# A fused FFN, attention, FFN block: a new order for the work of its opening

## The chip, the cores and the metric

The kernel runs on all 8 cores of one Trainium2 chip. Every core runs the same program on its own 2 of the 16 sequences, and the cores do not talk to each other. The metric is the device time in microseconds (us) of the slowest core. TensorE is called PE below, VectorE DVE, ScalarE ACT, GpSimd POOL; SP is the engine that issues most of the DMAs.

## What is computed

For x of 16 sequences of 2048 rows of 1024 (f32), with normalised rows h = layernorm(x):

```python
x = x + 0.5 * ffn(layernorm(x))      # ffn: h @ W_shared.T + w(h) * (h @ W_expert.T) + bias
x = x + attention(layernorm(x))      # 16 heads of 64, causal, softmax, output product Wp
x = x + 0.5 * ffn(layernorm(x))
```

In the FFN every row goes to two experts that share one matrix, so that the expert part is a scale per row (from a gate of 7 columns, softmax, top 2) times the same product. The scales of the two experts add up to 1, and the kernel multiplies with the sum of W_shared and W_expert.

## The kernel before

**Tiles and chunks.** A core has 4096 rows: 32 tiles of 128 rows, in 8 chunks of 4 tiles. Chunks 0 to 3 are one sequence, 4 to 7 the other. A tile is loaded (`ld`, SP), its statistics taken (`st`, DVE), its reciprocal deviation computed (`rt` for a tile, `r` for a chunk, ACT), the rows normalised (`a`, DVE or ACT), the FFN bias added to x (`xf`, POOL), and the normalised tile transposed (`t`: by PE with an evacuation copy for the first chunks, else by a DMA transpose that SP issues). Then come the gate (`ga`, `gb`), the FFN products (`f`, two halves of 512 columns to a tile), statistics of the new x (`s1`), the store of it (`sx`, SP), and the second normalisation and transposes (`a`, `t` with layer 1). A chunk's attention inputs are 8 products `q`, 8 `k` and 8 `v`; each is 8 matmuls of 512 columns, a DVE evacuation, and a store to memory. `n`, `b1` and `b2` make a bound for the exponent from the squares of q and k; the first attention step of a chunk can't do without it.

**Weights.** 48 pieces of 512 KB come through staging slots by SP (`wl`). Pieces 0 to 15 are pairs of FFN weights that DVE or POOL adds into WF (`ws`, 8 of them; 4 and 5 on POOL); pieces 16 to 23 are Wq, 24 to 31 Wk, 32 to 39 Wv, cast to bf16 by ACT or, for the numbers in `ON_POOL`, by POOL (`wc`). A slot's next piece is issued only when the last user of the slot is done, and that `wl` stands right behind the `ws` or `wc` in the order.

**One order for all engines.** `a_order` and `c_order` write out by hand the order of everything but attention; `make_order` puts the attention steps (`qd`), their loads (`al`), and the pieces of products around them (`pt` computes a product up to so many of its 8 matmuls) between them, by estimated costs of its own. Each engine walks through this one list `ORDER`, does the entries that are its own, and waits in line wherever an entry isn't ready. So an entry that waits on SP or DVE holds up all that stands behind it there. In the list `aux[k]` are the entries behind product k of a chunk (0 to 7 q, 8 to 15 k, 16 to 23 v). The attention loads `al` of units 0 to 3 stand ahead of the fifth q product of chunk 1, each as three DMAs, and wait for all q, k and v stores of chunk 0.

**Buffers.** Before the first attention step the products and PE transposes share 7 PSUM banks in turn; after it banks 6 and 7. q and k results go through 4 buffers `QKS`, v through 3 `VST`; each buffer waits for its last store to land. On ACT in chunk 0, each q or k store is issued before the cast that follows it in the list.

Of the kernel before, what the change touches and what calls it, by code (L numbers as in the profile page):

```python
# [17 lines left out]
DCN = 8  # L18
# [56 lines left out]

ON_POOL = (17, 19, 21, 23)


def ffn_order(l, i):
# [16 lines left out]
def a_order():  # L98

    o = [("ld", n) for n in range(4)] + [("bl", 0)] + [("wl", j) for j in range(8)]  # L100
# [3 lines left out]
    def one_cast():  # L104
        if cast:
            j = cast.pop(0)
            o.extend([("wc", j)] + [("wl", k) for k in range(40) if WPREV[k] == j])

    def ws(j):
        o.extend([("ws", j)] + [("wl", k) for k in range(40) if WPREV[k] == 2 * j or WPREV[k] == 2 * j + 1])  # L110
# [13 lines left out]
    o += [("pt", ("f", 0, n, 0), 6) for n in range(4)]  # L124
    o.append(("gb", 0, 0))
    ws(3)
    o += [("br", 1), ("br", 2)]
    for n in range(4):
        o += [("st", n + 4), ("rt", 0, n + 4), ("a", 0, n + 4)]
        if n:  # L130
            o.append(("f", 0, n - 1, 0))
    ws(4)
    o.append(("xf", 0, 4))
    ws(5)
    o += [("xf", 0, 5), ("f", 0, 3, 0), ("t", 0, 4), ("t", 0, 5), ("xf", 0, 6), ("t", 0, 6), ("xf", 0, 7), ("t", 0, 7)]
    o += [("s1", n, 0) for n in range(4)] + [("ga", 0, 1)]
    o += [("bb", r, h) for r in (1, 2) for h in range(2)]
    o += [("gb", 0, 1)] + [("f", 0, n, 0) for n in range(4, 8)]
    o += [("pt", ("f", 0, n, 1), 4) for n in range(4)]
    ws(6)  # L140
    o += [("pt", ("f", 0, n, 1), 6) for n in range(4)]
    ws(7)
    for n in range(4):
        o += [("f", 0, n, 1), ("s1", n, 1), ("rt", 1, n)]
        one_cast()
        if n < 3:
            o.append(("a", 1, n))
            one_cast()
    o += [("f", 0, 4, 1), ("f", 0, 5, 1), ("t", 1, 0), ("t", 1, 1), ("a", 1, 3)]
    one_cast()  # L150
    o += [("f", 0, 6, 1), ("t", 1, 2), ("t", 1, 3), ("f", 0, 7, 1)]
    one_cast()
    for i in range(NCHUNK):
        aux = {k: [] for k in range(24)}
        if i == 0:
            for t in range(4):
                aux[t] += [("s1", 4 + t, 0), ("s1", 4 + t, 1)]
                aux[6 + t] += [("a", 1, 4 + t), ("t", 1, 4 + t)]
                aux[12 + t].append(("ld", 8 + t))
            aux[4].append(("r", 1, 1))  # L160
            for n in range(8):
                aux[2 + n].append(("sx", 0, n))
        elif i == 1:
            for t in range(4):
                aux[4 + t].append(("st", 8 + t))
                aux[9 + t] += [("a", 0, 8 + t), ("xf", 0, 8 + t), ("t", 0, 8 + t)]
            aux[8].append(("r", 0, 2))
            for t in range(2):
                aux[6 + t].append(("ld", 12 + t))
                aux[13 + t].append(("st", 12 + t))  # L170
            aux[14].append(("ga", 0, 2))
            aux[15].append(("gb", 0, 2))
        elif i < 7:
            aux[1].append(("r", 1, i + 1))
            for t in range(4):
                aux[2 + t] += [("a", 1, 4 * i + 4 + t), ("t", 1, 4 * i + 4 + t)]
# [29 lines left out]
        for k, e in enumerate(order if i != 1 else order[:16]):  # L206
            o.append(e)
            one_cast()
            o += aux[k]
            if k == 9:  # L210
                o.append(("n", 0, i))
            if k == 17:
                o.append(("n", 1, i))
            if k == 19:
                o.append(("b1", i))
            if k == 21:
                o.append(("b2", i))
        if i == 1:

            v = order[16:]  # L220
            for t in range(4):
                n = 8 + t
# [205 lines left out]
ORDER = make_order()  # L428
# [11 lines left out]
EARLY = [0] * 8  # L440
_uses = [0] * 8
_banks = (6, 7, 0, 1, 2, 3, 4)
_turn = 0
for _e in ORDER:
    if _e[0] == "pt":
        _e = _e[1]
    if _e == ("qd", 0):
        EARLY = list(_uses)
        _banks = (6, 7)
    elif _e == ("oe", NUNIT - 1):  # L450
        _banks = (6, 7, 0, 1, 2, 3, 4, 5)
    if _e[0] in ("bb", "t", "ga", "f", "q", "k", "v", "n", "b2", "bc", "p") and not by_dma(_e) and _e not in SHARED:
        _b = _banks[_turn % len(_banks)]
        _turn += 1
        SHARED[_e] = (_b, _uses[_b])
        _uses[_b] += 1
ATTENDED = {_e for _e in ORDER[ORDER.index(("oe", NUNIT - 1)):] if _e in SHARED}

ON_DVE = {("t", 0, 4), ("t", 0, 5)} | {("t", 1, _n) for _n in range(4)}

ON_ACT = {("a", 0, _n) for _n in range(4, 8)} | {("a", 1, _n) for _n in range(3)}


XNUSE = {}
# [14 lines left out]
_n = [0, 0, 0]  # L479
# [16 lines left out]
def build_program():  # L496
# [22 lines left out]
    with contextlib.ExitStack() as st:  # L519
# [460 lines left out]
        def tensor_program(e):  # L980
# [68 lines left out]
            def product(en, upto):  # L1049

                kind = en[0]
                begin = done.get(en, 0)
                done[en] = upto
                if not begin:
                    bank_free(en)
# [8 lines left out]
                else:  # L1064
                    n, h = en[-2], en[-1]
                    i, t = divmod(n, 4)
# [7 lines left out]
                for dc in range(begin, upto):  # L1074
                    if kind == "f":
                        if en[1] == 0 and n == 0 and dc % 2 == 0:
                            summed(e, 4 * h + dc // 2)
                        a = xt(2 * en[1], i)[:, dc, t * 128:(t + 1) * 128]
                        b = WF[:, dc, h * 512:(h + 1) * 512]
# [367 lines left out]
```

How the kernel before makes its waits and increments, by code:

```python
        def filled(e, entry):  # L692
            b, m = SHARED[entry]
            e.wait_ge(p_sh[b], m + 1)
# [1 line left out]
        def read_out(e, entry):  # L696
            b, m = SHARED[entry]
            e.wait_ge(r_sh[b], m + 1)
# [1 line left out]
        def transposed(e, entry):  # L700
            if entry in TDMA:
                b, m = TDMA[entry]
                e.wait_ge(d_t[b], 16 * m)
            else:
                read_out(e, entry)
# [21 lines left out]
        def summed(e, j):  # L728
            e.wait_ge(v_ws, j + 1 - 2 * (j > 5) - (j - 3) * (3 < j < 6))
            if j > 3:
                e.wait_ge(g_ws, min(2, j - 3))
# [1 line left out]
        def sum_pieces(e, j):  # L734
            h, m = divmod(j, 4)
            a, b = 2 * j, 2 * j + 1
            for p in (a, b):
                e.wait_ge(d_wl[WSLOT[p]], 16 * (WUSE[p] + 1))
            return e.tensor_tensor(WF[:, 2 * m:2 * m + 2, h * 512:(h + 1) * 512],
                                   piece(a).rearrange("p (c f) -> p c f", c=2),
                                   piece(b).rearrange("p (c f) -> p c f", c=2), ALU.add)
# [1 line left out]
        def cast(e, j):  # L744
            m = sum(p <= j for p in ON_POOL)
            if j - 15 - m:
                e.wait_ge(a_wc, j - 15 - m)
            if m:
                e.wait_ge(g_wc, m)
# [1 line left out]
        def cast_piece(e, j, copy):  # L752
# [4 lines left out]
                cast(e, j - 1)
            e.wait_ge(d_wl[WSLOT[j]], 16 * (WUSE[j] + 1))
            return copy(dst, piece(j))
# [36 lines left out]
            def const(instr):  # L797
# [1 line left out]
                instr.then_inc(g_c, 1)  # L799
                n += 1
                e.wait_ge(g_c, n)
```

## Time and profile before

| | |
|---|---|
| time, median of 3 runs | 1239.21 us (1237.67 to 1243.95) |
| the profiled execution | time 1238.26 us, span of its slowest core 1236.7 us |
| spans of the 8 cores | 1225.8 to 1236.7 us; core 5 is the slowest, core 1 has 1232.7 |
| busy on that core | PE 93%, ACT 60%, DVE 56%, POOL 43% |

The span runs from a core's first to its last instruction; the time is 1.6 us above it. Products are matmuls at line 1091 of the kernel: `WF,XT` for the FFN, `XT,WQKV` for q and k (the moving operand is the transposed x), `WQKV,XT` for v. Line 1114 is a PE transpose, 1133 the gate, 1143 the sum of squares `n`, 1150 the matmul of `b2`, 1010, 1033 and 1041 are attention, 1171 are statistics, 1200 and 1328 the normalisation on DVE and ACT, 942 a DMA transpose, 904 the load of x, 897 the load of a weight piece, 910 the store of x.

### The profile page before, as it was taken

Reading aid. Unit: us, or ns where it says so; the run is one execution under the profiler, and the core shown is the slowest. Engines: PE = TensorE matmul, PEld = TensorE weight load, DVE = VectorE, ACT = ScalarE, POOL = GpSimd, SP = SyncE. Lnnn points to the kernel's source line nnn. Section 1 sums busy time; section 2 is a strip of 40 time slices with the busy share of each in tenths; the row PEclk is TensorE's granted clock in tenths of the full one; section 3 lists DMA queues with packets and bytes.
Section 4 is the critical chain, followed back from the end, with each engine's and each line's share of the span. In section 5 each row is a group of like instructions: output and inputs, shape, how many; then the busy total and the mean of one; then the engine's idle time right before and its main releaser. Section 6 shows DMA issues by size and latency. Waiting matters only on the chain.

```text
span 1236.7 us, 28817 instructions; the slowest of 8 cores (1225.8 to 1236.7 us)
## 1 busy us (share of the span) xinstructions
PE 1149.8 (93%) x9038; PEld 430.1 (35%) x9038; DVE 695.4 (56%) x1239; ACT 740.1 (60%) x937; POOL 531.7 (43%) x794
## 2 busy tenths in 40 slices
PE   4789887998999999999999999999989999999997
PEld 2334333332333333333333333333333333333343
DVE  6674678765555455544545545446655545455465
ACT  3362134466667676677667556667767777777711
POOL 5633554356035405603531534725536271716352
PEclk9899999998999999999999999999999999999999
DMA  8989659697357447537544646746666664847142
GB/s 278 323 268 280 158 108 190 149 238 198 90 134 217 118 127 213 122 128 157 151 128 129 148 118 173 207 115 171 133 190 165 212 175 143 215 110 240 26 162 86
DMA packets 206760, 206.93 MB, mean 167 GB/s; under 512 B 127251, under 2 KB 171795, under 8 KB 206614
## 3 DMA queue, kind: packets, MB, share of 16 engines
q1 hardware_dynamic: 198560, 200.85, 60.6%
q10 hardware_dynamic: 8054, 4.25, 1.3%
q8 instruction: 78, 1.28, 0.4%
q14 instruction: 68, 0.56, 0.2%
HBM read 117.23 MB, written 66.85 MB: 149 GB/s over the span
## 4 chain that ended last, share of the span: by engine, by line
PE 76%; DVE 9%; issue 5%; DMA 4%; SPq 2%; ACT 2%; DVEq 0%; ACTq 0%; POOL 0%; POOLq 0%
PE PS L1091 47%; PE PS L1033 11%; PE PS L1010 11%; PE PS L1041 4%; DMA XC<-x 2%; DVE BNS L1171 2%; PE PS L1155 1%; DVE VST L1253 1%; DVE ATT L1278 1%; SPq L942 1%; DMA XT<-XN 1%; DMA qd<-QKS 1%; DVE QKS L1242 1%; DVE DSB L1285 1%; DVE XC L1227 1%
## 5 line engine op out<-in xcount | busy, mean ns | idle before, releaser
L1382 ACT ACTIVATE PT<-PS,MB 128x1024 bf16<-128x1024 f32 (+3 forms) x428 | 401.2, 988 | 150.8 <-PE PS L1010 150.1
L855 POOL TENSOR_TENSOR SQ<-QKS 128x256 bf16<-128x256 bf16 x256 | 166.1, 671 | 232.4 <-DVE QKS L1242 199.1
L1091 PE MATMUL PS<-XT,WQKV 128*128 128x512 bf16 x1024 | 247.5, 387 | 9.5 <-DVE QKS L1242 7.2
L1091 PE MATMUL PS<-WF,XT 128*128 128x512 bf16 x1024 | 247.8, 387 | 2.5 <-DVE VST L1253 2.3
L1382 ACT ACTIVATE ATT<-PS,MB 128x1024 bf16<-128x1024 f32 x212 | 193.6, 964 | 70.0 <-PE PS L1010 69.9
L869 POOL TENSOR_TENSOR OTT<-OS,RR 128x256 bf16<-128x256 f32 x124 | 89.2, 739 | 326.4 <-ACT RR L1393 326.4
L1010 PE MATMUL PS<-ATT 64*128 64x512 bf16 (+3 forms) x1280 | 177.6, 350 | 1.6 <-ACT PT L1382 0.9
L825 POOL TENSOR_TENSOR XC<-XC,BF 128x256 f32<-128x256 f32 x192 | 135.5, 736 | 63.6 <-DVE XN L1200 63.6
L1091 PEld LDWEIGHTS PS<-XT,WQKV 128*128 128x128 bf16 x1024 | 92.6, 99 | 148.0 <-issue 56.3
L1091 PEld LDWEIGHTS PS<-WF,XT 128*128 128x128 bf16 x1024 | 92.8, 99 | 141.2 <-issue 49.9
L1091 PE MATMUL PS<-WQKV,XT 128*128 128x512 bf16 x512 | 122.8, 380 | 9.2 <-DVE VST L1253 8.1
L1227 DVE SCALAR_TENSOR_TENSOR XC<-PS,GG,XC 128x512 f32<-128x512 f32 x96 | 71.7, 749 | 92.7 <-PE PS L1091 92.0
L1033 PE MATMUL PS<-PT,ATT 128*32 128x512 bf16 (+3 forms) x1712 | 118.9, 354 | 0.2 <-DVE PT L1278 0.2
L1171 DVE BATCH_NORM_STATS2 BNS<-XC 128x6 f32<-128x512 f32 x156 | 104.4, 688 | 16.4 <-DMA XC<-x 7.3
L1010 PEld LDWEIGHTS PS<-ATT 64*128 64x128 bf16 x1280 | 45.9, 93 | 135.5 <-issue 133.4
L1242 DVE TENSOR_SCALAR QKS<-PS,BK 128x512 bf16<-128x512 f32 x64 | 48.0, 750 | 72.7 <-PE PS L1091 66.3
L1253 DVE TENSOR_TENSOR VST<-PS,BV 128x512 bf16<-128x512 f32 x64 | 44.0, 688 | 79.2 <-PE PS L1091 76.3
L1242 DVE TENSOR_SCALAR QKS<-PS,BQ 128x512 bf16<-128x512 f32 x64 | 47.8, 748 | 64.1 <-PE PS L1091 60.7
L1041 PE MATMUL PS<-PT,ONES 128*32 128x512 bf16 (+3 forms) x856 | 81.3, 350 | 0.0
L1391 ACT ACTIVATE RR<-PS 128x512 f32<-128x512 f32 x64 | 38.2, 597 | 70.3 <-PE PS L1155 69.6
L1091 PEld LDWEIGHTS PS<-WQKV,XT 128*128 128x128 bf16 x512 | 44.7, 97 | 76.7 <-issue 31.8
L1285 DVE CAST DSB<-PS 128x512 bf16<-128x512 f32 x64 | 44.2, 690 | 46.4 <-PE PS L1041 45.3
(107 smaller groups left out, 1080.0 us busy)
## 6 DMA issues: line engine op xcount, KB each, us to landing
XC<-x SPq DMA_DIRECT2D x30, 512.0 KB, 7.2
x1d<-XC SPq DMA_DIRECT2D x30, 512.0 KB, 5.3
XC<-x1d SPq DMA_DIRECT2D x18, 512.0 KB, 7.4
out<-XC SPq DMA_DIRECT2D x18, 512.0 KB, 3.4
ATT<-qd SPq DMA_DIRECT2D x64, 128.0 KB, 3.9
ATT<-kd SPq DMA_DIRECT2D x16, 512.0 KB, 5.5
ATT<-vd SPq DMA_DIRECT2D x16, 512.0 KB, 6.3
od<-OTT SPq DMA_DIRECT2D x62, 128.0 KB, 3.4
```

The costliest lines, as they stand in the source:

```text
L825: i = e.tensor_tensor(x[:, f:f + 256], x[:, f:f + 256], b[:, f:f + 256], ALU.add)
L855: i = e.tensor_tensor(SQ[:, m % 8, f], q[:, f], q[:, f], ALU.mult)
L869: m = e.tensor_tensor(to[:, f], OS[:, u % 2, f], RR[:, u % 2, f], ALU.mult)
L1010: i = e.matmul(PS[:, S_BANK + 2 * m + h, off:512], kk[64 * h:64 * h + 64, (j + m) * 128:(j + m + 1) * 128], q[64 * h:64 * h + 64, off:512] ...
L1033: e.matmul(PS[32 * g:32 * g + 32, O_BANK, off:512], vv[:, v + 32 * g:v + 32 * g + 32], ptile(k)[:, 2 * m + g // 2, off:512], start=(j + m ...
L1041: i = e.matmul(PS[32 * g:32 * g + 32, D_BANK, off:512], ONES[:, 0:32], ptile(k)[:, 2 * m + h, off:512], start=(j == 0 and (m == 0 or c > 0 ...
L1091: m = e.matmul(sbank(en), a, b, start=(dc == 0), stop=(dc == DCN - 1))
L1171: m = e.bn_stats(BNS[:, b, 6 * h:6 * h + 6], xtile(l, n)[:, h * 512:(h + 1) * 512])
L1227: i = e.scalar_tensor_tensor(x, sbank(en), GG[:, n // 4 % 2, n % 4:n % 4 + 1], x, ALU.mult, ALU.add)
L1242: was_read(e.tensor_scalar(QKS[:, m % NQK, :], sbank(en), bias[:, hp:hp + 1], None, ALU.add), en)
L1285: e.tensor_copy(DSB[:, u % 2, :], PS[:, D_BANK, :]).then_inc(v_ds, 1)
L1382: e.activation(ptile(k)[:, 2 * m:2 * m + 2, off:512], PS[:, S_BANK + 2 * m:S_BANK + 2 * m + 2, off:512], AF.Exp, bias=MB[:, u // HPN, hp % ...
```

## The change

The opening of `a_order` is written anew. FFN products of tiles 0 to 3 are issued whole as parts ahead of their evacuations; tiles 4 to 7 are normalised one by one between those (tiles 4 and 6 on ACT, 5 and 7 on DVE, instead of all four on ACT); the second halves of tiles 0 to 3 are begun as soon as their weights come, ahead of the gate and the first halves of tiles 4 to 7; casts 18 and 22 go to POOL. 8 casts stand ahead of the first q product instead of 9, and the first four q products have two casts behind each instead of one. The broadcasts `bb` of two bias rows move from the opening to products 10 to 13. The third chunk (tiles 8 to 11) is loaded three products sooner, its statistics move from q products 4 to 7 of chunk 1 to behind products 15, 17, 19 and 21 of chunk 0, its normalisation and DMA transposes from products 9 to 12 of chunk 1 to products 1 to 4, and its gate from product 14 to product 8. The loads of tiles 12 and 13 move from products 6 and 7 of chunk 1 to 20 and 22 of chunk 0, their statistics to products 10 and 12. Of the 7 PSUM banks the one whose last user ends first in the list is taken, not the next in turn.

```diff
--- before.py
+++ after.py
@@ -75,7 +75,7 @@
 
 
 
-ON_POOL = (17, 19, 21, 23)
+ON_POOL = (17, 18, 19, 21, 22, 23)
 
 
 def ffn_order(l, i):
@@ -124,52 +124,68 @@
     o += [("pt", ("f", 0, n, 0), 6) for n in range(4)]
     o.append(("gb", 0, 0))
     ws(3)
+
+    def parts(products, m):
+
+        o.extend(("pt", p, m) for p in products)
+
+    half = [("f", 0, n, 1) for n in range(4)]
+    parts([("f", 0, n, 0) for n in range(4)], 8)
     o += [("br", 1), ("br", 2)]
-    for n in range(4):
-        o += [("st", n + 4), ("rt", 0, n + 4), ("a", 0, n + 4)]
-        if n:
-            o.append(("f", 0, n - 1, 0))
+
+    o += [("st", 4), ("rt", 0, 4), ("a", 0, 4), ("xf", 0, 4), ("f", 0, 0, 0)]
+    o += [("st", 5), ("rt", 0, 5), ("t", 0, 4), ("f", 0, 1, 0), ("a", 0, 5), ("xf", 0, 5), ("t", 0, 5)]
+    o += [("st", 6), ("rt", 0, 6), ("a", 0, 6)]
     ws(4)
-    o.append(("xf", 0, 4))
+    o += [("f", 0, 2, 0), ("st", 7), ("rt", 0, 7), ("t", 0, 6), ("f", 0, 3, 0), ("a", 0, 7)]
     ws(5)
-    o += [("xf", 0, 5), ("f", 0, 3, 0), ("t", 0, 4), ("t", 0, 5), ("xf", 0, 6), ("t", 0, 6), ("xf", 0, 7), ("t", 0, 7)]
-    o += [("s1", n, 0) for n in range(4)] + [("ga", 0, 1)]
-    o += [("bb", r, h) for r in (1, 2) for h in range(2)]
-    o += [("gb", 0, 1)] + [("f", 0, n, 0) for n in range(4, 8)]
-    o += [("pt", ("f", 0, n, 1), 4) for n in range(4)]
     ws(6)
-    o += [("pt", ("f", 0, n, 1), 6) for n in range(4)]
+    o += [("xf", 0, 6), ("t", 0, 7), ("s1", 0, 0), ("s1", 1, 0)]
+    parts(half, 2)
+    o += [("ga", 0, 1), ("xf", 0, 7)]
     ws(7)
-    for n in range(4):
-        o += [("f", 0, n, 1), ("s1", n, 1), ("rt", 1, n)]
+    parts(half, 4)
+    parts(half, 6)
+    o += [("s1", 2, 0), ("s1", 3, 0), ("gb", 0, 1)]
+    parts(half, 8)
+    one_cast()
+    one_cast()
+    parts([("f", 0, 4, 0), ("f", 0, 5, 0)], 8)
+
+    o += [("f", 0, 0, 1), ("s1", 0, 1), ("rt", 1, 0), ("a", 1, 0)]
+    o += [("f", 0, 1, 1), ("s1", 1, 1), ("rt", 1, 1), ("t", 1, 0)]
+    one_cast()
+    parts([("f", 0, 6, 0)], 8)
+    o += [("f", 0, 2, 1), ("s1", 2, 1), ("a", 1, 1), ("rt", 1, 2), ("a", 1, 2)]
+    one_cast()
+    o += [("f", 0, 3, 1), ("s1", 3, 1), ("rt", 1, 3), ("t", 1, 1)]
+    parts([("f", 0, 7, 0)], 8)
+    o += [("t", 1, 2), ("a", 1, 3), ("t", 1, 3)]
+    for k in range(4):
         one_cast()
-        if n < 3:
-            o.append(("a", 1, n))
-            one_cast()
-    o += [("f", 0, 4, 1), ("f", 0, 5, 1), ("t", 1, 0), ("t", 1, 1), ("a", 1, 3)]
-    one_cast()
-    o += [("f", 0, 6, 1), ("t", 1, 2), ("t", 1, 3), ("f", 0, 7, 1)]
-    one_cast()
+    o += [("f", 0, n, 0) for n in range(4, 8)] + [("f", 0, n, 1) for n in range(4, 8)]
     for i in range(NCHUNK):
         aux = {k: [] for k in range(24)}
         if i == 0:
             for t in range(4):
                 aux[t] += [("s1", 4 + t, 0), ("s1", 4 + t, 1)]
+                aux[10 + t].append(("bb", 1 + t // 2, t % 2))
                 aux[6 + t] += [("a", 1, 4 + t), ("t", 1, 4 + t)]
-                aux[12 + t].append(("ld", 8 + t))
+                aux[9 + t].append(("ld", 8 + t))
+                aux[15 + 2 * t].append(("st", 8 + t))
             aux[4].append(("r", 1, 1))
             for n in range(8):
                 aux[2 + n].append(("sx", 0, n))
+            aux[20].append(("ld", 12))
+            aux[22].append(("ld", 13))
         elif i == 1:
+            aux[0].append(("r", 0, 2))
             for t in range(4):
-                aux[4 + t].append(("st", 8 + t))
-                aux[9 + t] += [("a", 0, 8 + t), ("xf", 0, 8 + t), ("t", 0, 8 + t)]
-            aux[8].append(("r", 0, 2))
+                aux[1 + t] += [("a", 0, 8 + t), ("xf", 0, 8 + t), ("t", 0, 8 + t)]
+            aux[8].append(("ga", 0, 2))
+            aux[9].append(("gb", 0, 2))
             for t in range(2):
-                aux[6 + t].append(("ld", 12 + t))
-                aux[13 + t].append(("st", 12 + t))
-            aux[14].append(("ga", 0, 2))
-            aux[15].append(("gb", 0, 2))
+                aux[10 + 2 * t].append(("st", 12 + t))
         elif i < 7:
             aux[1].append(("r", 1, i + 1))
             for t in range(4):
@@ -206,6 +222,8 @@
         for k, e in enumerate(order if i != 1 else order[:16]):
             o.append(e)
             one_cast()
+            if k < 4:
+                one_cast()
             o += aux[k]
             if k == 9:
                 o.append(("n", 0, i))
@@ -440,8 +458,9 @@
 EARLY = [0] * 8
 _uses = [0] * 8
 _banks = (6, 7, 0, 1, 2, 3, 4)
-_turn = 0
-for _e in ORDER:
+_ends = {_e: _n for _n, _e in enumerate(ORDER)}
+_until = list(range(-8, 0))
+for _n, _e in enumerate(ORDER):
     if _e[0] == "pt":
         _e = _e[1]
     if _e == ("qd", 0):
@@ -450,15 +469,16 @@
     elif _e == ("oe", NUNIT - 1):
         _banks = (6, 7, 0, 1, 2, 3, 4, 5)
     if _e[0] in ("bb", "t", "ga", "f", "q", "k", "v", "n", "b2", "bc", "p") and not by_dma(_e) and _e not in SHARED:
-        _b = _banks[_turn % len(_banks)]
-        _turn += 1
+        _b = min(_banks, key=lambda b: _until[b])
+        assert _until[_b] < _n
         SHARED[_e] = (_b, _uses[_b])
         _uses[_b] += 1
+        _until[_b] = _ends[_e]
 ATTENDED = {_e for _e in ORDER[ORDER.index(("oe", NUNIT - 1)):] if _e in SHARED}
 
-ON_DVE = {("t", 0, 4), ("t", 0, 5)} | {("t", 1, _n) for _n in range(4)}
-
-ON_ACT = {("a", 0, _n) for _n in range(4, 8)} | {("a", 1, _n) for _n in range(3)}
+ON_DVE = {("t", 0, 7), ("t", 1, 3)}
+
+ON_ACT = {("a", 0, 4), ("a", 0, 6), ("a", 1, 0), ("a", 1, 2)}
 
 
 XNUSE = {}
@@ -1050,6 +1070,8 @@
 
                 kind = en[0]
                 begin = done.get(en, 0)
+                if begin == DCN:
+                    return
                 done[en] = upto
                 if not begin:
                     bank_free(en)
```

## Rows read from the trace of the kernel before

**Rows 1.** Windows: us, busy (instructions) of PE, PEld, DVE, ACT, POOL; clock; DMA

```profile
0.00:123.00 123.00, 92.28 (x503) 43.06 (x504) 76.01 (x135) 49.67 (x85) 55.77 (x90) 0.93 0.96 289
123.00:240.00 117.00, 98.62 (x675) 40.39 (x674) 86.14 (x157) 38.76 (x70) 52.86 (x78) 0.97 0.68 148
...
400.00:600.00 200.00, 194.93 (x1624) 67.82 (x1624) 103.30 (x187) 139.37 (x160) 71.82 (x106) 1.00 0.57 152
```

**Rows 2.** PE's timeline: start, length, work [idle before and who ended it]

```profile
22.66 9.48 PE L1091 MATMUL PS<-WF,XT 128*128 128x512 bf16 x32
...
33.84 0.61 PE L1114 MATMUL PS<-IDE,XN 128*128 128x128 bf16 x8 [1.69 <-ACT XN L1328]
...
45.14 18.87 PE L1091 MATMUL PS<-WF,XT 128*128 128x512 bf16 x80
...
75.22 13.98 PE L1091 MATMUL PS<-XT,WQKV 128*128 128x512 bf16 x64
91.24 5.30 PE L1091 MATMUL PS<-XT,WQKV 128*128 128x512 bf16 x16 [2.05 <-ACT WQKV L760]
...
108.49 3.61 PE L1091 MATMUL PS<-WQKV,XT 128*128 128x512 bf16 x16 [0.93 <-ACT WQKV L760]
...
123.00 15.70 PE L1091 MATMUL PS<-XT,WQKV 128*128 128x512 bf16 x72
```

**Rows 3.** Timeline of SP's queue: start, time that the issues took

```profile
86.10 0.33 SPq L897 DMA_DIRECT2D ATT<-wtv  x1
...
107.35 2.61 SPq L904 DMA_DIRECT2D XC<-x  x4
127.56 0.33 SPq L934 DMA_DIRECT2D ATT<-qd  x1
...
134.53 0.83 SPq L904 DMA_DIRECT2D XC<-x  x2
```

**Rows 4.** DMA landing, us: 105-112 (x), 60-150 (x), 90-101 and 147-161 (transposes)

```profile
XC<-x SPq DMA_DIRECT2D x4, 512.0 KB, 11.7
...
DMA to landing us min/median/max: 6.2/9.5/12.5
...
XT<-XN SPq DMA_TRANSPOSE x3, 7.6
...
XT<-XN SPq DMA_TRANSPOSE x4, 3.1
```

**Rows 5.** PE's timeline at the start of attention and at the third chunk's gate

```profile
142.68 0.62 PE L1143 MATMUL PS<-SQ,BD 128*32 128x512 bf16 x8 [0.59 <-DVE QKS L1242]
146.37 0.81 PE L1091 MATMUL PS<-XT,WQKV 128*128 128x512 bf16 x3 [3.07 <-DVE QKS L1242]
...
166.32 0.34 PE L1133 MATMUL PS<-WGT,XT 128*128 128x7 bf16 x8 [3.58 <-DMA XT<-XN]
```

**Rows 6.** POOL's timeline in the opening

```profile
36.87 2.36 POOL L740 TENSOR_TENSOR WF<-WP 128x1024 bf16<-128x1024 f32 x1 [10.60 <-DMA WP<-wte]
39.18 2.56 POOL L825 TENSOR_TENSOR XC<-XC,BF 128x256 f32<-128x256 f32 x4
...
60.26 1.04 POOL L760 CAST WQKV<-WP 128x1024 bf16<-128x1024 f32 x1 [2.40 <-DMA WP<-wtq]
```

**Rows 7.** DVE's timeline: statistics of a tile, a v evacuation, the end of `b1`

```profile
77.89 1.28 DVE L1171 BATCH_NORM_STATS2 BNS<-XC 128x6 f32<-128x512 f32 x2
...
110.48 0.69 DVE L1253 TENSOR_TENSOR VST<-PS,BV 128x512 bf16<-128x512 f32 x1 [2.06 <-PE PS L1091]
...
117.49 0.26 DVE L1264 TENSOR_SCALAR DG<-IDE,NV 128x128 bf16<-128x128 bf16 x1
```

**Rows 8.** Window of PE alone: us, busy, granted clock, DMA share, GB/s

```profile
148.00:150.00 2.00, 2.00 (x6) 0.50 0.67 131
```

**Rows 9.** Waits of PE on core 1, 136 to 170 us: total, times, longest

```profile
PE PS L1133 <- DMA XT<-XN: 1.8, 1, 1.8
...
PE PS L1091 <- DVE QKS L1242: 0.5, 1, 0.5
```

## The prediction

> **What bounds the kernel now.** I read the table of stretches first [rows 1]. From 400 to 600 us PE is busy for 194.9 of 200 us at full clock; that is the state of nearly all of the kernel, and the change leaves it alone. Only two stretches have room: 0 to 123 us, where PE is busy for 92.3 us at a mean clock of 0.93 while the DMA engines are busy for 96%, and 123 to 240 us, where PE loses 18.4 us and DVE is busy for 74%. Because everything later is one list without slack on PE, what is won or lost on PE by 240 us should come out at the end, one for one. Next PE's own timeline [rows 2]: FFN products end their first batch at 32.1 us and go on at 45.1; between, PE does four transposes and little else. q products start at 75.2, k products wait 2.05 us for a cast, v products 0.93 us, and chunk 1 begins at 123.0 (call it S; its 72 matmuls are the 8 q products and the first k product). The third view is the queue of SP with its landings [rows 3, 4]: the loads of the third chunk's x are issued from 107.4 us only, behind the last two weight pieces (86.1), the stores of x and four DMA transposes, and they take 11.7 us to land. The fourth is PE after 138 us [rows 5].
>
> **Opening, 32 to 75 us.** Nothing of the FFN is removed; the question is how early PE gets at the second halves. They need the sum of pieces 8 and 9 on POOL, which came at 36.9 + 2.4 = 39.2 [rows 6]. In the new order two bias adds of 2.56 us stand ahead of it. Tile 4 is normalised when PE starts its transpose at 33.8 [rows 2], as now, so the sum ends at 33.7 + 2 x 2.56 + 2.36 = 41.2. From about 41.9, when the last of the four transposes is through, PE has 96 matmuls before q, 96 x 0.216 (13.98 / 64 less the pipeline's tail, [rows 2]) = 20.7 us; four transposes of 0.61, 2.4; the gate, 1.4; as much half clock as before, 1.6 (80 matmuls took 18.87 us for 80 x 0.216 = 17.3); and about 1.2 us behind the DVE copy of tile 7, which now stands behind a weight sum whose piece lands near 43.4 (landings run from 36.9 for piece 9 to 60.3 for piece 23, 1.67 us apiece [rows 6]). Sum 69.3: q starts 5.9 us sooner. The Wq pieces are in by 61.3, so they don't bind. Casts 18 and 22 on POOL cost 1.04 us each there; POOL has nothing due until the first squares, so nothing.
>
> **k and v, 75 to 109 us.** The last Wk cast is the eighth behind a q product instead of the seventh, in pairs of 2 x 1.04 us [rows 6] and 0.33 for the store's issue [rows 3]. With the first q result evacuated at 71.9, four such groups of 2.4 us end at 81.6, before k can start at 83.2 (69.3 + 13.9). That removes the 2.05 us, and what followed it: 16 matmuls took 5.30 us at low clock where 16 later took 3.61 [rows 2], 1.7 us. The v wait of 0.93 goes too. The four `bb` matmuls now cost about 1 us of dense PE time. So v can start at 108.5 - 5.9 - 3.7 - 0.9 + 1 = 99.0, up to 1.7 us later if the squares of q are late (their stores now wait behind cast pairs). Alone that would be 9.5 us. If nothing took it back, this would be the result.
>
> **What takes it back: x of the third chunk.** The statistics of tiles 8 to 11 now stand on DVE among v's evacuations, and each waits for its tile. Their loads stand in SP's queue behind two weight pieces, the stores of x and the transposes. Before, from the first weight piece (issued 86.1) to the loads (107.4) that queue took 21.2 us, since DMA was full. Now it starts near 78, when cast 28 is done, has one more 0.5 MB store (1.7 us), and so issues the first load near 97 (it has moved ahead of the last transpose) and the others at 100 to 103; with 9 to 11.7 us to land [rows 4], tile 9 is there at 110 to 113. Then DVE has, in this order: statistics of tile 9, 1.5; the `n` evacuation, 0.7; two v evacuations, 1.4; statistics of tile 10, 1.5; `b1`, 0.9 [rows 7]: 6.0 us. PE stands at `b2`, which it reaches 6 products and an `n` after v's start, at about 110, until 116 to 119. Two v products later, 3.5 us [rows 2], chunk 1 starts: tile 9 + 9.7 = 119.7 to 122.7, plus 1.8 us for the low clock after a wait of this length (as above). Middle 122.5, against 123.0. Bounds: the shortest landing of 6.2 us [rows 4] on an issue at 101.3, no clock loss: 117.2; the longest, 12.5 us on 103, with it: 127. The opening's gain is waited away for all but 0.5 us.
>
> **Start of attention.** Before, PE lost there 1.0 + 0.6 + 3.1 us waiting for k evacuations held up by q stores that landed late beside attention's loads and 1 MB of x [rows 3, 5], then 3.6 us for the last transposed tile of the third chunk at the gate, and after either a stretch at half clock [rows 8], 1.6 and 1.9 us. Together 11.8 us. The change takes the x loads away, but puts the DMA transpose of tile 11 right behind the 12 loads of `al`, which took SP from 127.56 to 134.5, 6.9 us [rows 3]. Tile 10 is normalised at S + 8.7 (four products of 1.73, the evacuation, 0.75, and the pass over the tile, 0.8), `al` is issued from S + 9.9 to S + 16.8, tile 11's transpose after it, at about S + 17. The gate now stands behind the first k product: PE is there at S + 15.7 [rows 2]. What a DMA transpose takes to land the trace shows from both sides, 3.1 us in a quiet stretch and 7.6 in a full one [rows 4]; I take 5.5, between, since `al` is still draining: S + 22.5. PE idles 6.8 us there, and at half clock loses another 1.7. In this time the stores of q land, so the old waits vanish within it: 8.5 us lost for 11.8, on this core 3.3 us better (bounds: +5.7 with 3.1 us, +1.2 with 7.6 us). On core 1 the same waits were 0.5 and 1.8 us [rows 9], some 3 us with its others: that core gets 5.7 us worse, ending at 1232.7 + 5.7. The slowest of eight is thus near 1238 from the one side and 1236.7 - 3.3 from the other; I count this part as +0.5 us (worse), with bounds of -5 and +5. The Trainium skill, DMA: Bandwidth & Descriptors, in the table of Latency and other measured facts, gives DMA transposes 261 GB/s. By it tile 11's 256 KB would be an estimated 1.0 us of transfer and the stall about 4 us shorter than mine; the 7.6 us of the trace's full stretch speak against using it while other transfers queue.
>
> **After that.** The squares of k, the gate's DVE work and two bias adds no longer meet attention's first steps; I count -1 us, out of the waits of 1 us and less there. The statistics of tiles 12 and 13 cost the same 1.5 us each wherever they stand.
>
> **Sum.** Against this execution's 1238.3 us: opening and v -0.5, attention's start +0.5, rest -1: 1237.3. The median of the three runs is 0.95 above that execution: 1238.2, which I give as 1238. What a measurement can tell from no change is about 0.5%, 6.2 us.
>
> **Rivals.**
> *The gains stay* (chance 0.30). The x tiles land with the bounds' 6 us, and tile 11's transpose in 3: 5.8 + up to 5 + 1 = some 11 us, or half of each, 7: 1228 to 1232. For it: SP's queue starts 8 us sooner. Against: four transposes and the stores still have to go through a full DMA.
> *A new wait decides, slower* (0.24). The gate's wait for tile 11: if its transpose lands more than 9 us after issue, behind `al` and q stores, PE idles over 10 us; with S no sooner than before, cores such as 1 end 9 us late: 1247. It decides from a stall of about 11 us on, 4 more than I forecast; the two waits for x add to it if tile 9 lands after 116.
> *The change of order does nothing at all for q* (inside my forecast): if PE starts q at 75 as before, v at about 104 still waits for x, and the time stays within 2 us of the forecast.
> My own case, within 0.5%, has 0.46; its own range is 1233 to 1244. For 8 in 10 both signs must be let in: 1229 to 1246.
>
> **What would show it.** Right: q at 68 to 71 us, no wait on a cast ahead of k, PE idle for over 5 us ahead of the `b2` matmul with DVE waiting for the load of x; then a gate waiting 5 to 9 us on a DMA transpose ahead of the first scores. Wrong: v evacuations that never wait for x (then S is near 113 and the time near 1228), or the gate passing without a wait.

## The result, and the profile after

The changed kernel takes 1245.58 us (median of 20 runs) where the kernel before takes 1240.01 (20 runs). The ratio is 1.0052, with a 95% interval of 1.0033 to 1.0071: slower by half a per cent. (Medians are over all runs; ratios and intervals leave out runs in which the cores of a die ran at a lower granted clock, so a ratio is not exactly the quotient of the two medians beside it.) The time is just inside the outer range of the forecast (1229 to 1246), outside the range of its own case (1233 to 1244), and the direction is not the one it gave: it had 1238 and a sum 1 us below its base.

The profiled execution took 1247.8 us, its slowest core (core 2) 1246.3. The table of stretches of that core, in the columns of [rows 1] (which show core 5 of the kernel before):

```profile
0.00:123.00 123.00, 89.43 (x500) 41.70 (x501) 83.03 (x147) 46.77 (x78) 61.93 (x92) 0.93 0.97 298
123.00:240.00 117.00, 100.74 (x674) 40.86 (x673) 78.14 (x142) 37.84 (x69) 52.07 (x78) 0.93 0.61 138
```

DVE has 7 us more to do ahead of 123 us and 8 us less behind it, as the statistics moved; PE has done no more by then. Its timeline on that core shows why; the rows answer to [rows 2] and [rows 5]:

```profile
42.40 3.62 PE L1113 MATMUL PS<-WF,XT 128*128 128x512 bf16 x8
...
69.70 17.43 PE L1113 MATMUL PS<-XT,WQKV 128*128 128x512 bf16 x80
...
99.67 3.62 PE L1113 MATMUL PS<-WQKV,XT 128*128 128x512 bf16 x16
103.22 0.62 PE L1165 MATMUL PS<-SQ,BD 128*32 128x512 bf16 x8
103.77 7.08 PE L1113 MATMUL PS<-WQKV,XT 128*128 128x512 bf16 x32
118.46 0.26 PE L1172 MATMUL PS<-DG,ONES 128*128 128x128 bf16 x1 [7.61 <-DVE DG L1286]
118.58 5.27 PE L1113 MATMUL PS<-WQKV,XT 128*128 128x512 bf16 x16
123.69 15.70 PE L1113 MATMUL PS<-XT,WQKV 128*128 128x512 bf16 x72
139.23 0.75 PE L1155 MATMUL PS<-WGT,XT 128*128 128x7 bf16 x24
146.76 0.36 PE L1155 MATMUL PS<-WGT,XT 128*128 128x7 bf16 x8 [6.78 <-DMA XT<-XN]
```

q starts at 69.7 instead of 75.2 us and v at 99.7 instead of 108.5, without a wait on a cast. Then PE stands 7.6 us ahead of the `b2` matmul, runs the next two v products at half clock (5.27 us for 16 matmuls instead of 3.62), and starts chunk 1 at 123.7, where the kernel before started it at 123.0. Behind the first k product it stands 6.8 us at the gate. What held up `b2` is on DVE's timeline:

```profile
104.10 1.29 DVE L1193 BATCH_NORM_STATS2 BNS<-XC 128x6 f32<-128x512 f32 x2 [2.76 <-DMA XC<-x]
105.49 0.21 DVE L1196 BATCH_NORM_AGGREGATE MV<-BNS 128x2 f32<-128x12 f32 x1
105.66 1.29 DVE L1275 TENSOR_TENSOR VST<-PS,BV 128x512 bf16<-128x512 f32 x2
112.35 1.29 DVE L1193 BATCH_NORM_STATS2 BNS<-XC 128x6 f32<-128x512 f32 x2 [5.40 <-DMA XC<-x]
...
118.06 0.25 DVE L1286 TENSOR_SCALAR DG<-IDE,NV 128x128 bf16<-128x128 bf16 x1
```

The statistics of tile 8 wait 2.8 us for x, those of tile 9 another 5.4, and the last step of `b1` comes 5.7 us behind the start of tile 9's. And what held up the gate is on SP's:

```profile
78.43 1.27 SPq L917 DMA_DIRECT2D ATT<-wtv  x2
...
97.54 0.34 SPq L924 DMA_DIRECT2D XC<-x  x1
97.98 2.13 SPq L962 DMA_TRANSPOSE XT<-XN  x1
100.27 1.57 SPq L930 DMA_DIRECT2D x1d<-PT  x1
101.99 3.00 SPq L924 DMA_DIRECT2D XC<-x  x5
128.98 5.29 SPq L962 DMA_TRANSPOSE XT<-XN  x3
134.77 0.59 SPq L954 DMA_DIRECT2D ATT<-qd  x1
...
140.80 1.84 SPq L962 DMA_TRANSPOSE XT<-XN  x1
```

Three transposes go out ahead of attention's loads, the fourth only at 140.8, behind all twelve; it lands 5.8 us later (a row of the DMA issues from 138 to 145 us has 5.8).

All cores show both waits: 5.1 to 7.6 us ahead of `b2`, 5.6 to 6.8 us at the gate. That cores 2 and 3 are the slowest (1246.3 and 1244.2 us; the other six are between 1229.1 and 1234.8) goes with a later wait, behind the second mark below. Because a stall on one core of one execution is partly chance, the marks below are means over the eight cores of one profiled execution each, read from PE's timelines: the start of chunk 1, and the `b2` matmuls of chunks 1 and 2.

| kernel | chunk 1 starts | `b2` of chunk 1 | `b2` of chunk 2 |
|---|---|---|---|
| before | 123.2 | 190.0 | 311.3 |
| changed | 123.5 | 192.0 | 314.0 |

So the profile shows 0.3 us lost by the start of chunk 1, 1.7 more by the next mark, and 0.7 more by the third. These marks are exact for their execution and rough for the kernel: over the 75 runs of the kernel before that the ratios of the experiments use, the mean of a run's eight spans scatters by 2.1 us (standard deviation).

### The profile page after: what moved, and what is told of

Read it like the earlier page. It is cut to its first block, busy times and chain, and to the rows that moved or that the text cites. A ratio compares the mean times of both kernels' runs of the same rounds, so it can differ in the third digit from the quotient of the medians.

```text
span 1246.3 us, 28809 instructions; the slowest of 8 cores (1229.1 to 1246.3 us)
## 1 busy us (share of the span) xinstructions
PE 1151.6 (92%) x9038; PEld 430.2 (35%) x9038; DVE 697.2 (56%) x1238; ACT 737.0 (59%) x930; POOL 536.4 (43%) x796
## 4 chain that ended last, share of the span: by engine, by line
PE 73%; DVE 10%; DMA 6%; issue 5%; SPq 3%; ACT 2%; DVEq 0%; ACTq 0%; POOL 0%; POOLq 0%
PE PS L1113 44%; PE PS L1053 11%; PE PS L1030 11%; PE PS L1061 4%; DMA XC<-x 2%; DVE BNS L1193 2%; PE PS L1177 1%; SPq L962 1%; DMA ATT<-wte 1%; DVE VST L1275 1%; DVE XN L1222 1%; DMA ATT<-vd 1%; DVE ATT L1300 1%; DVE QKS L1264 1%; DVE DSB L1307 1%
## 5 line engine op out<-in xcount | busy, mean ns | idle before, releaser
L1404 ACT ACTIVATE ATT<-PS,MB 128x1024 bf16<-128x1024 f32 x212 | 193.6, 964 | 67.5 <-PE PS L1030 67.2
L1113 PE MATMUL PS<-WQKV,XT 128*128 128x512 bf16 x512 | 127.3, 390 | 7.8 <-DVE VST L1275 7.6
L1053 PE MATMUL PS<-PT,ATT 128*32 128x512 bf16 (+3 forms) x1712 | 119.3, 355 | 2.9 <-DVE PT L1300 2.8
## 6 DMA issues: line engine op xcount, KB each, us to landing
ATT<-qd SPq DMA_DIRECT2D x64, 128.0 KB, 4.4
od<-OTT SPq DMA_DIRECT2D x62, 128.0 KB, 3.5
```

The source lines that it names most:

```text
L1053: e.matmul(PS[32 * g:32 * g + 32, O_BANK, off:512], vv[:, v + 32 * g:v + 32 * g + 32], ptile(k)[:, 2 * m + g // 2, off:512], start=(j + m ...
L1113: m = e.matmul(sbank(en), a, b, start=(dc == 0), stop=(dc == DCN - 1))
L1404: e.activation(ptile(k)[:, 2 * m:2 * m + 2, off:512], PS[:, S_BANK + 2 * m:S_BANK + 2 * m + 2, off:512], AF.Exp, bias=MB[:, u // HPN, hp % ...
```

## The experiments

Ratios are to the kernel before, over interleaved runs on one chip for each of three groups, with 95% intervals: experiments 1, 2, 5 and 6; 3, 8, 10 and 11; 4, 7, 9 and 12. The changed kernel's 1.0052 is from runs of its own, so a comparison across groups goes by ratios only. All but experiment 9 have the new choice of PSUM banks, experiment 2 too. That choice was not tried by itself, nor were the parts of the new opening other than its cast pairs.

**1. The new opening alone.** The third chunk and tiles 12 and 13 go back to where they were:

```diff
-                aux[9 + t].append(("ld", 8 + t))
-                aux[15 + 2 * t].append(("st", 8 + t))
+                aux[12 + t].append(("ld", 8 + t))
...
-            aux[0].append(("r", 0, 2))
...
-                aux[1 + t] += [("a", 0, 8 + t), ("xf", 0, 8 + t), ("t", 0, 8 + t)]
-            aux[8].append(("ga", 0, 2))
...
+                aux[4 + t].append(("st", 8 + t))
+                aux[9 + t] += [("a", 0, 8 + t), ("xf", 0, 8 + t), ("t", 0, 8 + t)]
+            aux[8].append(("r", 0, 2))
...
+            aux[14].append(("ga", 0, 2))
```

> The new opening, the cast pairs and the bias broadcasts behind products 10 to 13, but the third chunk (loads, statistics, normalisation, transposes, gate) and tiles 12 and 13 where the kernel before had them. My theory is that the opening brings PE 9 us and that the statistics of the third chunk among v's evacuations wait them away: then v starts near 99 us, no wait ahead of the b2 matmul, chunk 1 near 114 instead of 123, and the time is 6 to 9 us below the kernel before, ratio near 0.994. Rival: what PE gains in the opening is given back wherever the next transfer is late (attention's loads, the q stores), whatever the statistics do: then chunk 1 starts near 114 but the time is within 3 us of the kernel before. Second rival: the opening itself is at fault for the slower time: ratio 1.003 or more.

Measured: 0.9945 (0.992 to 0.9969), 1230.66 us against 1235.94. PE's timeline of its slowest core, core 4:

```profile
67.71 19.22 PE L1112 MATMUL PS<-XT,WQKV 128*128 128x512 bf16 x80
...
100.53 3.62 PE L1112 MATMUL PS<-WQKV,XT 128*128 128x512 bf16 x16
...
111.54 0.22 PE L1171 MATMUL PS<-DG,ONES 128*128 128x128 bf16 x1
111.60 3.62 PE L1112 MATMUL PS<-WQKV,XT 128*128 128x512 bf16 x16
115.05 15.70 PE L1112 MATMUL PS<-XT,WQKV 128*128 128x512 bf16 x72
```

v starts as in the changed kernel (100.5), nothing stands ahead of `b2`, and chunk 1 starts at 115.1, on the mean of the cores at 114.8. The opening is not at fault; it is worth 6.8 us of the time by this ratio (3.8 to 9.9 by its interval), and the rest of the change costs more than that.

**2. The third chunk alone**, with the old opening, single casts and the old places of the `bb`; the loads of tiles 12 and 13 move too, and the new choice of banks is in:

```diff
-                aux[12 + t].append(("ld", 8 + t))
+                aux[9 + t].append(("ld", 8 + t))
+                aux[15 + 2 * t].append(("st", 8 + t))
...
+                aux[1 + t] += [("a", 0, 8 + t), ("xf", 0, 8 + t), ("t", 0, 8 + t)]
+            aux[8].append(("ga", 0, 2))
```

> The old opening and single casts with the third chunk moved as in the changed kernel, gate and all. Theory: the loads of x leave the queue of SP at about 103 to 108 us as before, land by 112 to 119, PE stands ahead of b2 for 3 to 7 us, chunk 1 starts at 127 to 130, and the gate wait of 6 to 7 us on tile 11's transpose comes on top: 8 us or so slower than the kernel before, ratio 1.005 to 1.009. Rival: the moved third chunk is harmless without the earlier opening, since the loads then have time to land: ratio 0.998 to 1.002.

Measured: 1.0091 (1.0058 to 1.0123). The waits of PE from 60 to 260 us on core 1:

```profile
PE PS L1138 <- DMA XT<-XN: 8.0, 2, 7.1
PE PS L1155 <- DVE DG L1269: 4.7, 1, 4.7
```

(A total takes in other waits of the line; the longest is the one of the gate.) Both waits are there without the new opening, 3.3 to 6.2 us ahead of `b2` and 4.8 to 7.1 at the gate; chunk 1 starts at 125.3 to 131.0. The third chunk's moves cost about 9 thousandths, and the two halves of the change nearly add up: 0.9945 and 1.0091 against 1.0052 measured for both, 1.0036 by multiplication.

**3. Statistics among v's evacuations, alone** on top of experiment 1 (loads three products sooner, nothing else of the third chunk):

```diff
-                aux[12 + t].append(("ld", 8 + t))
+                aux[9 + t].append(("ld", 8 + t))
+                aux[15 + 2 * t].append(("st", 8 + t))
...
-                aux[4 + t].append(("st", 8 + t))
```

> The new opening alone, plus only the three products sooner loads of tiles 8 to 11 and their statistics behind products 15, 17, 19 and 21 of chunk 0; normalisation, transposes and gate stay where they were. Theory: this alone makes PE wait 5 to 7 us ahead of b2 and starts chunk 1 at 121 to 126 us, so that the 6 to 7 us that the opening brings are gone: ratio to before 0.999 to 1.002. Rival: the wait costs less than it shows, because statistics done early take 6 us of DVE work away from the q products and attention's start: ratio 0.996 or less.

Measured: 1.0013 (0.9991 to 1.0035). PE waits 4.4 to 6.9 us ahead of `b2` on all cores and chunk 1 starts at 121.8 to 128.0. The gain of the opening is gone with this one edit, as expected.

**4. x three products sooner still**, in the changed kernel:

```diff
-                aux[9 + t].append(("ld", 8 + t))
+                aux[6 + t].append(("ld", 8 + t))
```

> The changed kernel with the loads of tiles 8 to 11 another three products sooner (behind products 6 to 9 of chunk 0, among the stores of x and the DMA transposes), so that x is in earlier and the transposes of tiles 4 to 7 later. Theory (PE stands ahead of b2 because x lands late behind a full queue): the wait of 5 to 7.6 us there shrinks to 1 to 4 us and chunk 1 starts at 118 to 121 us; the gate's wait stays at 6 us; ratio to before 1.001 to 1.003. Rival (DVE's own work on statistics among v's evacuations is the limit, not the landing): the wait ahead of b2 stays above 5 us and the time is the changed kernel's.

Measured: 1.0027 (0.9995 to 1.0058). The wait ahead of `b2` is gone on all cores, not only shrunk: it was the landing of x, not DVE's own work. But chunk 1 starts at 114.7 to 123.8, the late ones being 123.1 and 123.8 on cores 4 and 5. A new wait stands there ahead of the sum of squares `n`, 1.0 to 2.8 us on six cores, 3.3 and 6.1 on these two (at most 1.1 in the changed kernel); on core 5, in PE's and DVE's timelines:

```profile
110.98 1.04 PE L1165 MATMUL PS<-SQ,BD 128*32 128x512 bf16 x8 [6.07 <-POOL SQ L875]
...
100.59 0.75 DVE L1264 TENSOR_SCALAR QKS<-PS,BK 128x512 bf16<-128x512 f32 x1 [4.58 <-DMA kd<-QKS]
```

DVE waits there for stores of k to land before it can evacuate the next product. And the wait at the gate grew, from 5.6 to 6.8 us to 5.5 to 9.2, and this is the longest group of PE's waits from 60 to 260 us on core 7:

```profile
PE PS L1155 <- DMA XT<-XN: 11.1, 2, 9.0
```

**5. and 6. The gate's wait.** In one kernel the gate goes back behind product 14, in the other the normalisation and transposes of tiles 8 to 11 go to products 0 to 3, ahead of attention's loads:

```diff
-            aux[8].append(("ga", 0, 2))
-            aux[9].append(("gb", 0, 2))
+            aux[14].append(("ga", 0, 2))
+            aux[15].append(("gb", 0, 2))
```

```diff
-                aux[1 + t] += [("a", 0, 8 + t), ("xf", 0, 8 + t), ("t", 0, 8 + t)]
+                aux[t] += [("a", 0, 8 + t), ("xf", 0, 8 + t), ("t", 0, 8 + t)]
```

> The changed kernel with the gate of the third chunk back behind product 14 of chunk 1 (and its DVE part behind 15). Theory: the 5.6 to 6.8 us that PE stands at the gate are gone, since tile 11's transpose lands at about 22 us after the start of chunk 1 and PE comes to the gate 5 us after that; the first k evacuations wait for q stores by 2 to 4 us instead; time 2 to 5 us below the changed kernel, ratio to the kernel before near 1.002. Rival: the wait is only moved, to the k evacuations behind late q stores, and the time stays as the changed kernel's, ratio 1.005.

> The changed kernel with the normalisation and the DMA transposes of tiles 8 to 11 one product sooner (products 0 to 3 of chunk 1), so that all four transposes stand in SP's queue ahead of attention's first 12 loads. Theory (the transpose of tile 11 is late because it stands behind those loads): the gate waits at most 1 us, the first scores wait 0 to 2 us for their loads, and the time is 3 to 5 us below the changed kernel, ratio to before 1.001 to 1.003. Rival (the transposes are slow because DMA is busy with the q stores and x, not because of their place): the gate still waits 4 us or more, time as the changed kernel's.

Measured: 1.0017 (0.9998 to 1.0037) and 1.0028 (1.0006 to 1.005). With the gate late no core waits for it ahead of attention. With the transposes one product (1.7 us) sooner, and by it ahead of the loads in SP's queue, the wait is 0 on six cores and 0.5 and 1.7 us on two, 6.0 us less on the mean: most of tile 11's lateness was its place in the queue. Against the changed kernel's 1.0052 they take 4.3 and 3.0 us off, with intervals that still touch its own; that is half to two thirds of the wait removed. Other waits come up behind it: the first scores wait 0.4 to 3.0 us for attention's loads in the one, and 0.4 to 2.8 us for these or for a q evacuation in the other. The waits of PE from 60 to 260 us, of core 2 of the second kernel:

```profile
PE PS L1165 <- POOL SQ L875: 3.4, 2, 2.8
...
PE PS L1030 <- DMA ATT<-vd: 2.4, 1, 2.4
PE PS L1030 <- DVE GD L1229: 2.3, 1, 2.3
```

Here the first scores wait for their own loads, 2.4 us.

**7. Both of these together.**

> The changed kernel with both repairs of the gate: transposes of tiles 8 to 11 ahead of attention's loads, and the gate behind product 14. Theory: each took away the same 6 us wait, so together they give little more than one: the wait ahead of b2 stays, chunk 1 starts at 119 to 125 us, ratio to before 0.999 to 1.002. Rival: the two add up (3.5 and 2.4 thousandths below the changed kernel): ratio 0.999 or less.

Measured: 1.001 (0.9989 to 1.003), no gate wait, still 3.7 to 7.7 us ahead of `b2`, chunk 1 at 120.0 to 125.2. It can't be told from either alone; the two do not visibly add up. The first scores now wait 2.6 to 6.5 us, 3.6 on the mean against 1.9 and 1.5 with either alone.

**8. Single casts** in the kernel of experiment 1:

```diff
-            if k < 4:
-                one_cast()
```

> The new opening alone with one cast behind every q product instead of two behind each of the first four. Theory: the last Wk cast comes 3 to 4 us after PE is ready for k, PE waits that long and runs at half clock behind it; v waits again by about 1 us; 4 to 6 us of the opening's gain gone, ratio to before 0.998 to 1.000. Rival: the loads of the last two Wv pieces and DMA set the pace anyway, and the time is the opening's alone, 0.9945.

Measured: 1.0009 (0.999 to 1.0028). On core 7, PE's timeline:

```profile
67.80 13.98 PE L1110 MATMUL PS<-XT,WQKV 128*128 128x512 bf16 x64
89.16 6.17 PE L1110 MATMUL PS<-XT,WQKV 128*128 128x512 bf16 x16 [7.38 <-ACT WQKV L777]
...
112.36 6.52 PE L1110 MATMUL PS<-WQKV,XT 128*128 128x512 bf16 x16 [4.32 <-ACT WQKV L777]
```

On this core, the slowest, the waits are far above what I expected, 7.4 and 4.3 us, and both are followed by half clock; the k wait is 7.8 us on core 6 and 3.4 to 4.3 on the other six, as expected. Chunk 1 starts at 122.5 to 129.8 over the cores, and the time is just above the range that I gave. The new opening needs the pairs: without them no gain can be told.

**9. The pairs alone** in the kernel before:

```diff
             one_cast()
+            if k < 4:
+                one_cast()
             o += aux[k]
```

> The kernel before with one edit: two casts behind each of the first four q products of chunk 0, and nothing of the new opening. Theory (PE waits for the last Wk cast whatever the opening): the k wait of 2.05 us with the half clock behind it and the v wait of 0.93 go, chunk 1 starts at 118 to 119 us instead of 123, ratio to before 0.996 to 0.998. Rival: with q at 75 us the pieces of Wk and Wv have only just landed and the pairs only delay the q stores: ratio 0.999 to 1.001.

Measured: 0.998 (0.9956 to 1.0004), chunk 1 at 116.8 to 126.5. The cast wait went and another came: on core 4 PE waits 3.6 and 2.4 us for the squares of q and k. The first of them follows a q evacuation that stands 3.8 us on DVE until a q store lands; that the pairs on ACT delayed that store is likely, not shown. Inconclusive by its interval; by the single values of experiments 1, 8 and 9, opening and pairs are worth 5.5 thousandths together, the pairs alone 2 and the opening alone nothing.

**10. Loads of tiles 12 and 13 away from attention's**, on top of experiment 1:

```diff
+            aux[20].append(("ld", 12))
+            aux[22].append(("ld", 13))
...
-                aux[6 + t].append(("ld", 12 + t))
```

> The new opening alone, and the loads of tiles 12 and 13 behind products 20 and 22 of chunk 0 instead of behind q products 6 and 7 of chunk 1, nothing else. Theory: 1 MB less beside attention's loads and the q stores; the first k evacuations wait less for q stores, by 1 to 3 us on the slower cores: ratio to before 0.992 to 0.9945. Rival: PE's waits at attention's start are hidden or come from attention's own loads: no difference to the opening alone.

Measured: 0.9944 (0.9914 to 0.9974), the ratio of the opening alone. My theory gave 0.992 to 0.9945 and does not tell itself from its rival by that; but the waits that were to shrink did not: the first scores wait 1.0 to 3.6 us where experiment 1 has 0.5 to 1.0. The rival holds: this part brings nothing that can be told.

**11. The third chunk early, but not among v**, on top of that: loads at 9 + t, statistics behind q products 0 to 3 of chunk 1, transposes behind 5 to 8.

```diff
-                aux[12 + t].append(("ld", 8 + t))
+                aux[9 + t].append(("ld", 8 + t))
...
-                aux[4 + t].append(("st", 8 + t))
-                aux[9 + t] += [("a", 0, 8 + t), ("xf", 0, 8 + t), ("t", 0, 8 + t)]
-            aux[8].append(("r", 0, 2))
+                aux[t].append(("st", 8 + t))
+                aux[5 + t] += [("a", 0, 8 + t), ("xf", 0, 8 + t), ("t", 0, 8 + t)]
+            aux[3].append(("r", 0, 2))
```

> The new opening alone (as in the first experiment), and the third chunk earlier but not among v: its loads where the changed kernel has them, its statistics behind the first four q products of chunk 1, its normalisation and transposes behind products 5 to 8, its gate at 14 as before; loads of tiles 12 and 13 behind products 20 and 22 of chunk 0. Theory: chunk 1 still starts near 114 us with no wait ahead of b2, the gate's wait of 1 to 3 us goes, and the first k evacuations wait less: 1 to 3 us below the opening alone, ratio to before 0.992 to 0.994. Rival: any earlier third chunk collides with the q and k stores and attention's loads, and the time is the opening's alone or above: 0.995 or more.

Measured: 0.9986 (0.9965 to 1.0007). My theory missed; the rival was right. Chunk 1 starts at 113.1 to 119.3 (mean 117.1, 2.3 us behind experiment 1), the gate never waits, and more of the gain goes at the first scores, which wait 5.4 to 6.9 us on seven cores, here on core 5:

```profile
116.32 15.70 PE L1113 MATMUL PS<-XT,WQKV 128*128 128x512 bf16 x72
137.46 0.93 PE L1030 MATMUL PS<-ATT 64*128 64x512 bf16 x4 [5.44 <-DVE QKS L1264]
```

DVE's timeline there has v's last evacuations waiting 5.4 us for a v store to land, then four statistics between q evacuations, and then a q evacuation waiting 2.7 us for a q store; the scores' banks are read out only after it.

**12. One product sooner.** The kernel of experiment 10 with `r` at 7 instead of 8 and the tiles' normalisation and transposes at 8 + t instead of 9 + t:

```diff
-                aux[9 + t] += [("a", 0, 8 + t), ("xf", 0, 8 + t), ("t", 0, 8 + t)]
-            aux[8].append(("r", 0, 2))
+                aux[8 + t] += [("a", 0, 8 + t), ("xf", 0, 8 + t), ("t", 0, 8 + t)]
+            aux[7].append(("r", 0, 2))
```

> An attempt at a better version: the new opening alone with the loads of tiles 12 and 13 early (as in the experiment before), and the normalisation and transposes of tiles 8 to 11 one product sooner, behind products 8 to 11 of chunk 1. Theory: the gate's wait of 0.8 to 2.5 us shrinks by 1 to 1.7 us, nothing else moves: ratio to before 0.993 to 0.995, at the edge of what can be told from the version without it. Rival: DVE meets the first k evacuations, and the first scores wait more: 0.996 or more.

Measured: 0.9906 (0.9875 to 0.9937), 1227.84 us against 1238.74: faster than both kernels, the lowest ratio of the study, and below the range that I gave. The gate's wait, 0.8 to 2.5 us without it, is gone on all cores, and chunk 1 starts at 113.6 to 116.2. But the marks do not explain a better time: on the mean of the cores chunk 1 starts at 114.8 and its `b2` and that of chunk 2 come at 179.8 and 302.2, where experiment 1 has 114.8, 179.0 and 299.0 and experiment 10 has 115.4, 180.8 and 302.0; the first scores wait up to 5.0 us. It was on another chip than experiments 1 and 10, and the intervals overlap: that it beats either is not shown.

## Why the forecast was wrong by its direction

All that I had named as signs of being right came: q at 68 to 71, no cast wait, both long waits with the cause that I gave. The signs were waits, and the forecast failed on what they cost.

*Opening:* right. q at 69.3 forecast, 69.7 measured; no cast wait; v at 99.0 forecast, 99.7 measured. (On the mean of the cores v starts 8.6 us sooner, against 9.5.)

*x of the third chunk:* right in mechanism and size. Loads from 97 and to 103 forecast, 97.5 and up to 105 issued; `b2` until 116 to 119, measured 114.2 to 120.0; chunk 1 at 122.5, measured 123.5 on the mean. Experiments 1, 3 and 4 show the cause from both sides. The term was -0.5 us, measured +0.3.

*Gate:* the wait itself was right, 6.8 us forecast, 5.6 to 6.8 measured, and its cause, the place behind attention's loads, is shown by experiment 6. The transpose took 5.8 us to land where I had taken 5.5. The Trainium skill, DMA: Bandwidth & Descriptors, Latency and other measured facts, gives DMA transposes with a non-contiguous middle dimension 261 GB/s, by which this one would take an estimated 1.0 us; what PE waits for is the whole time from issue to landing, nearly six times that.

*The step that failed* is the price of attention's start, "I count this part as +0.5 us (worse)". I had set a relief of 3.3 us on core 5 (span 1236.7) against a loss of 5.7 us on core 1 (1232.7) and taken a value between. Both single numbers were near: from the start of chunk 1 to the `b2` of chunk 1, core 5 won 2.1 us (71.0 to 69.0) and core 1 lost 4.1 (63.4 to 67.5). But the time is that of the slowest core, and no value between is: by my own numbers core 1 would end at 1238.4, 1.7 us above 1236.7. And I had priced two cores of eight. Core 5 was the slowest partly because it had the longest waits there in that execution, 4.1 us on k evacuations and 3.6 at the gate; core 2, only 0.2 us shorter, lost 3.2 us. The mean core lost 1.7. Its two parts can be told apart: from the start of chunk 1 to its `b2` the mean is 66.8 us before, 64.2 and 63.8 in experiments 1 and 3, which leave the transposes and the gate where they were, and 68.5 in the changed kernel. So the relief was some 2.9 us, and the early transposes and gate cost 4.6 (the loads of tiles 12 and 13 are in that). Experiment 1 has nearly all of the relief with nothing of the third chunk moved, so it did not come from the x loads taken away, as I had it. The times agree: from experiment 3 (1.0013) to the changed kernel (1.0052) it is 4.8 us, where I had +0.5 and -1 for all behind the start of chunk 1.

*"After that", -1 us,* was wrong in sign: the means lose another 0.7 us by the third mark. On cores 2 and 3 a k evacuation near 285 us waits long for a q store; this row of core 2's PE is the longest wait behind the gate:

```profile
286.76 0.58 PE L1177 MATMUL PS<-DSB,SEL 128*128 128x512 bf16 x1 [4.69 <-DVE QKS L1264]
```

These are the two cores that ended last, 9 us or more behind the others. Before, no core waited over 2.3 us there. Experiments 4, 7, 11 and 12 have such waits of 3.3 to 5.3 us on two cores each, 8 and 10 one of 3.1 and 3.9, experiment 1 none over 1.7; in experiment 12 the time is the lowest all the same. The traces point at SP's queue. On the eight cores of all fourteen traces where such a wait is over 4 us, the four DMA transposes that SP issued between 235 and 275 us held its queue for 10.9 to 13.3 us in all; on the other 104 cores all such transposes took 10.3 us or less, but for one with 11.9 us and a wait of 3.8. The eight are four pairs of neighbouring cores (2 and 3, 4 and 5, 6 and 7 twice). Why the issues take so long on them was not tried, so this is a correlation.

*Ratio against marks.* The ratio says 6.4 us, the marks 2.7. The mean of the eight spans in the two profiled executions differs by 2.5 us (1232.8 and 1235.2), as the marks do. But the execution of the kernel before was a slow one by this measure: over its 75 runs beside the experiments the mean is 1230.1, and only 5 of them reach 1232.8. Over 18 runs of the changed kernel it is 1236.1, 6.0 us more (these were not interleaved with the 75). So the missing microseconds are most likely those between an untypical execution and the usual one, not those of a stretch, and the size of each term above carries this error of some 3 us. By ratios the account nearly closes: the opening 0.9945, the statistics among v up to 1.0013, the gate's wait 3.5 or 2.4 thousandths more, against 1.0052.

*Luck.* The forecast's outer range holds the time only by its width. The rival "a new wait decides, slower" had 1247, near what came, but by a stall of 11 us and a transpose landing over 9 us after its issue; measured were 6.8 and 5.8.

*Parts without effect:* the loads of tiles 12 and 13 (experiment 10) were counted into the relief at attention's start, and bring nothing that can be told.

## What to carry to other kernels

Work that PE gains in a stage is worth what the next transfer in line allows: before moving anything earlier, write down when its data land and which in-order queue it then blocks. Here four statistics moved among evacuations cost the whole gain of a new opening, and a transpose behind twelve loads in SP's queue cost half to two thirds of the 6 us that PE waited for it, while the plain opening with nothing else moved was faster. Price an edit on every core, not from the waits of the slowest one, and remember that the slowest core after it can be another. One profiled execution is one draw: compare its spans with those of the other runs before building on its waits. Test a change of several moves one by one: of the parts of this one, the opening with its cast pairs was worth 5.5 thousandths, the loads of tiles 12 and 13 nothing that can be told, and the statistics and the gate's wait cost about 7 and 3.

## What the runs showed of the hardware

After each wait of 5 us and more in the changed kernel PE ran at the lower of its clock levels for some microseconds, on all eight cores: the 16 matmuls behind `b2` took 5.3 to 6.4 us instead of 3.6. PE's windows on core 2, in columns busy, clock, DMA share, GB/s:

```profile
114.00:116.00 2.00, 0.00 (x0) 0.79 1.01 346
116.00:118.00 2.00, 0.00 (x0) 0.50 1.05 266
118.00:120.00 2.00, 1.54 (x5) 0.50 0.22 51
120.00:122.00 2.00, 2.00 (x7) 0.51 0.60 131
122.00:124.00 2.00, 2.00 (x11) 1.00 0.00 0
...
148.00:150.00 2.00, 2.00 (x6) 0.50 0.00 0
150.00:152.00 2.00, 2.00 (x9) 0.50 0.00 0
```

A clock of 0.50 is 1.2 GHz of 2.4. It fell while PE stood still (from 110.9 to 118.5 us). Behind the 6.8 us at the gate it lasted until 152 us, 8 matmuls taking 3.60 us instead of 1.9, so that this wait cost over 2 us more than its own length, where I had counted 1.7.

After shorter waits it is not settled by their length. In the kernel before, every core waited 2.0 to 2.9 us for the last Wk cast. Behind it the 16 matmuls took 5.30 us on cores 3 and 5 [rows 2], and 3.61, full clock, on cores 0, 1, 6 and 7, core 0 after the longest wait of all:

```profile
92.63 3.61 PE L1091 MATMUL PS<-XT,WQKV 128*128 128x512 bf16 x16 [2.91 <-ACT WQKV L760]
```

So the 1.7 us that the prediction took for this were again those of core 5, not of the mean core.

The issue of one DMA transpose occupied SP's queue for 1.2 us in some places and for up to 6.6 us in others (core 2 of the changed kernel, at 250.7 us), and the DMAs behind it in that queue were issued only after it.
